# Eleven stages on one core: small weights in one tensor, matrix copies on two engines, deeper buffers in three projections

## The reference

```python
h = tok_mix(x)                 # q,k,v = x@W + b; y = ((d_gamma * (q@k.T)) @ v) @ Wo + bo; prelu. d_gamma 1024x1024
h = concatenate([h, txt], axis=1)
h = h + attention8(ln(h))      # 8 heads of 8, relative bias, softmax, projection with bias
h = h + experts16(ln(h))       # y = z + top 2 of 16 relu experts, layer norm with gamma and beta
h = h + linear_attn(ln(h))     # elu(q)+1, elu(k)+1, projection with bias
u = ln(h)                      # then rms norm, rope, causal attention (4 heads of 16)
u = u + causal(u) @ wo.T
h = h + u + experts8(rms(u))   # top 2 of 8 gated experts
```

## Time and profile before

| | us |
|---|---|
| median of 3 runs | 2847.63 |
| lowest and highest | 2846.12, 2851.1 |
| the profiled execution | 2844.59 |
| its span, first to last instruction | 2842.8 |

### The profile page before, as it was taken

One profiled execution on the slowest core, in us unless ns is written; L12 is line 12 of the kernel. 1 busy time (PEld: TensorE's weight loads), 2 busy tenths in 40 slices (PEclk: granted clock), 3 DMA queues, 4 the chain that ended last, 5 costly groups with the idle time before them and its releaser, 6 DMA issues. The chain is left out here.

```text
span 2842.8 us, 52541 instructions
## 1 busy us (share of the span) xinstructions
PE 2499.5 (88%) x18456; PEld 1092.8 (38%) x18456; DVE 1983.2 (70%) x5070; ACT 1519.3 (53%) x2629; POOL 400.8 (14%) x500
## 2 busy tenths in 40 slices
PE   5988657999999999997499999896679999599999
PEld 3323552333333333333333333564544444423333
DVE  5777667888888888883377776657676765266665
ACT  2331663777777777775144444334656667143443
POOL 1011210000000000002312111222100100411110
PEclk9998666999999999998599999665689999599999
DMA  2101751111111111122500100134441222701100
GB/s 75 23 15 24 239 203 58 48 48 32 48 46 34 48 41 39 48 45 48 111 12 19 25 15 21 48 94 125 154 139 61 81 62 57 155 12 30 30 21 15
DMA packets 272791, 174.02 MB, mean 61 GB/s; under 512 B 225857, under 2 KB 230786, under 8 KB 271282
## 3 DMA queue, kind: packets, MB, share of 16 engines
q1 hardware_dynamic: 262170, 151.59, 19.9%
q0 software_dynamic: 10368, 19.06, 2.2%
HBM read 96.11 MB, written 74.53 MB: 60 GB/s over the span
## 5 line engine op out<-in xcount | busy, mean ns | idle before, releaser
L1674 DVE TENSOR_REDUCE att_mpart<-ps 128x1 f32<-128x512 f32 x1024 | 635.6, 683 | 82.2 <-PE ps L1494 52.0
L1642 ACT ACTIVATE att_p<-ps 128x704 f32<-128x704 f32 x768 | 543.7, 760 | 136.1 <-PE ps L1558 131.8
L1587 PE MATMUL ps<-att_p,att_v 128*9 128x352 f32 x3072 | 300.5, 462 | 0.1
L1494 PE MATMUL ps<-att_kT,att_qT 64*128 64x512 bf16 x1024 | 276.4, 387 | 20.7 <-DMA att_qz<-qt_d 8.3
L1558 PE MATMUL ps<-att_qm,att_kT 64*128 64x352 bf16 x1536 | 251.9, 317 | 10.4 <-ACT att_p L1642 8.0
L1288 DVE TENSOR_REDUCE cau_mpart<-ps 128x1 f32<-128x512 f32 (+5 forms) x384 | 193.4, 552 | 80.3 <-PE ps L1114 60.9
L2419 ACT ACTIVATE mo_act<-ps,mo_b 128x768 f32<-128x768 f32 x176 | 156.3, 901 | 132.4 <-PE ps L2301 126.9
L2572 DVE TENSOR_TENSOR mo_g<-mo_act,ps 128x768 f32<-128x768 f32 x176 | 167.4, 951 | 77.8 <-PE ps L2336 41.2
L1255 ACT ACTIVATE cau_p<-ps 128x704 f32<-128x704 f32 (+6 forms) x272 | 171.5, 660 | 81.7 <-PE ps L1173 49.7
L2971 ACT ACTIVATE mo_act<-ps 128x1024 f32<-128x1024 f32 (+1 forms) x108 | 102.9, 953 | 195.0 <-PE ps L2885 194.8
L1558 PEld LDWEIGHTS ps<-att_qm,att_kT 64*128 64x128 bf16 x1536 | 82.8, 93 | 287.5 <-issue 278.0
(11 more groups left out here) (444 smaller groups left out, 4257.0 us busy)
## 6 DMA issues: line engine op xcount, KB each, us to landing
qs_d<-pre_qs SPq DMA_DIRECT2D x8, 1152.0 KB, 4.4
att_qs<-qs_d SPq DMA_DIRECT2D x32, 288.0 KB, 4.1
qt_d<-pre_qT SPq DMA_DIRECT2D x8, 1056.0 KB, 4.4
kt_d<-pre_kT SPq DMA_DIRECT2D x8, 1056.0 KB, 7.4
att_kT<-kt_d SPq DMA_DIRECT2D x32, 264.0 KB, 2.7
att_qT<-qt_d SPq DMA_DIRECT2D x32, 264.0 KB, 3.1
cqt_d<-cpr_qT SPq DMA_DIRECT2D x8, 1056.0 KB, 4.4
cau_qT<-cqt_d SPq DMA_DIRECT2D x16, 528.0 KB, 4.0
```

Source lines behind the costliest of these rows:

```text
L1494: mm = pe.matmul(ps[:, bank, :], qT[half(s), u, j * P:(j + 1) * P], kT[half(s), u, c * BANK:(c + 1) * BANK], start=True, stop=not near)
L1587: mm = pe.matmul(ps[32 * cg:32 * cg + DV, 7, 0:TH], v[:, u, i, s, :], p[:, r, s, :], start=i < 2, stop=i == FULL - 1)
L1642: e = act.activation(p[:, n % PRING, :, :], ps[:, bank:bank + 2, 0:TH], ACT.Exp)
L1674: red = dve.tensor_reduce(mpart[:, j, s, c:c + 1], ps[:, bank, :], AX.X, ALU.max)
```

## The change

The small weights of the token mix come as one tensor of 128 x 324 and are, like the wide q and k weights, asked for by ACT; SP begins with the rows of image 0 and the matrix. The unit matrices are written in POOL's part of the first stage, and PE waits for them. PE turns four parts of the matrix between the first products, and nine of the sixteen copies are made by ACT. The splitting of x on ACT is cut in two pieces. The copy of txt is issued after the load of image 2.

```diff
+        small = nm.sb("small", [P, W_ALL])
+        wvT, bvb, wo = small[0:C, 0:P], small[0:C, P:2 * P], small[0:C, 2 * P:2 * P + C]
+        bqk, bo, slope = (small[:, 2 * P + C + i:2 * P + C + j] for i, j in ((0, 2), (2, 3), (3, 4)))
...
-        NW = 16 * 12
+        NW = 16 * 2
+
+        ACT_GT = (4, 5, 6, 7, 8, 9, 11, 13, 15)
+
+        def copied(eng, x_):
+
+            if x_ in ACT_GT:
+                eng.wait_ge(S["gt_cp_act"], sum(1 for i in ACT_GT if i <= x_))
+            else:
+                eng.wait_ge(S["gt_cp"], sum(1 for i in range(x_ + 1) if i not in ACT_GT))
...
-            sp.dma_start(wvT[:, :], a["L0_tok_WvT2"]).then_inc(S["w_in"], 16)
-            sp.dma_start(wo[:, :], a["L0_tok_Wo"]).then_inc(S["w_in"], 16)
-            sp.dma_start(bvb[:, :], a["L0_tok_bv_cols"]).then_inc(S["w_in"], 16)
...
-                sp.dma_start(wf[half, 0:V0], a["L0_tok_wqqkk"]).then_inc(S["w_in"], 16)
-                sp.dma_start(bqk[half, 0:1], a["L0_tok_bq"].rearrange("(c o) -> c o", o=1)).then_inc(S["w_in"], 16)
-                sp.dma_start(bqk[half, 1:2], a["L0_tok_bk"].rearrange("(c o) -> c o", o=1)).then_inc(S["w_in"], 16)
-                sp.dma_start(bo[half, :], a["L0_tok_bo"].rearrange("(c o) -> c o", o=1)).then_inc(S["w_in"], 16)
-            sp.dma_start(slope[:, :], a["L0_tok_prelu_a"].broadcast_to([P, 1])).then_inc(S["w_in"], 16)
...
-            sp.dma_start(h_img[:, TX:N, :], a["txt"]).then_inc(S["txt_out"], 16)
...
             load(2, 0)
+            sp.dma_start(h_img[:, TX:N, :], a["txt"]).then_inc(S["txt_out"], 16)
...
+            build_constants(pool, const)
             tidy(pool, const)
             front(0, 0)
...
-            pe.wait_ge(S["w_in"], NW)
-            pe.matmul(ps[:, 4, 0:C], wvT[:, :], wo[:, :], start=True, stop=True)
...
-            for _, part in front_parts:
-                part(0, 0)
-
-            for x_, n in enumerate(GT):
+            def turn_matrix(x_):
...
-                    pe.wait_ge(S["gt_cp"], x_ - 3)
+                    copied(pe, x_ - 4)
...
-            pe.wait_ge(S["gt_cp"], NS)
+
+            pe.wait_ge(const["made"], 2)
+            pe.wait_ge(S["w_in"], NW)
+            pe.matmul(ps[:, 4, 0:C], wvT, wo, start=True, stop=True)
+            pe.matmul(ps[:, 4, C:2 * C], bvb, wo, start=True, stop=True).then_inc(S["wv_mm"], 1)
+            x_turn(0, 0)
+            turn_matrix(0)
+            turn_matrix(1)
+            pe.wait_ge(S["wc_made"], 2)
+            for i in range(4):
+                qk(i)(0, 0)
+                if i < 2:
+                    turn_matrix(2 + i)
+            values(0, 0)
+            for x_ in range(4, NS):
+                turn_matrix(x_)
+            for x_ in range(NS - 4, NS):
+                copied(pe, x_)
             scores(0, 0, 0, False)
...
+            act.dma_start(small[:, :], a["L0_tok_small"]).then_inc(S["w_in"], 16)
+            act.dma_start(wf[:, 0:V0], a["L0_tok_wqqkk"]).then_inc(S["w_in"], 16)
...
+            def copy_matrix(x_):
...
+                act.wait_ge(S["gt_mm"], x_ + 1)
+                act.activation(gamT[:, n // 2, (n % 2) * BANK:(n % 2 + 1) * BANK], ps[:, x_ % 4, :], ACT.Identity)\
+                    .then_inc(S["gt_cp_act"], 1)
...
+
+            split_hi(0, 0)
...
             act.activation(wC[0:C, :], wf[0:C, :], ACT.Identity).then_inc(S["wc_made"], 1)
+            split_mid(0)
             act.wait_ge(S["wr_made"], 1)
...
             front(0, 0)
-            split(1, 1)
+            split_hi(1, 1)
+            for x_ in ACT_GT[:6]:
+                copy_matrix(x_)
+            split_mid(1)
+            for x_ in ACT_GT[6:]:
+                copy_matrix(x_)
...
+            copy_matrix(0)
+            copy_matrix(1)
+            for i in range(4):
+                rest(i)(0, 0)
+                if i < 2:
+                    copy_matrix(2 + i)
+            for i in range(4):
+                stack(i)(0, 0)
+            values(0, 0)
+            for x_ in range(4, NS):
+                if x_ not in ACT_GT:
+                    copy_matrix(x_)
+            copied(dve, NS - 1)
+            copied(dve, NS - 2)
```

```diff
+    OB, RB = 3, 4
...
-            if NO == 2:
-                at_least(sp, S["sum_made"], b - 1)
-            else:
-                at_least(sp, S["ot_mm"], b - 1)
+        def load(eng, b):
+            arrived_heads(eng, b)
+            at_least(eng, S["sum_made" if NO == 2 else "ot_mm"], b - OB + 1)
             for r0, r1 in parts:
-                sp.dma_start(o[r0:r1, par, :, :], o_d[bass.ds(b, 1), :, r0:r1, :].rearrange("b e r n -> r (b e) n"))\
-                    .then_inc(o_in[par], 16)
-
-        def load_rows(sp, b, par):
+                eng.dma_start(o[r0:r1, b % OB, :, :], o_d[bass.ds(b, 1), :, r0:r1, :].rearrange("b e r n -> r (b e) n"))\
+                    .then_inc(o_in[b % OB], 16)
+
+        def sums_in(eng, b):
+            eng.wait_ge(o_in[b % OB], 16 * len(parts) * (b // OB + 1))
+
+        def load_rows(sp, b):
             bi = bass.ds(b, 1)
-            at_least(sp, S["hn_made"], (b - 1) * 2)
-            sp.dma_start(res[:, par, 0:FULL, :], res_b[bi, 0:TX, :].rearrange("b (t p) c -> p (b t) c", p=P)).then_inc(res_in[par], 16)
-            sp.dma_start(res[0:TT, par, FULL, :], res_b[bi, TX:N, :].rearrange("b n c -> (b n) c")).then_inc(res_in[par], 16)
+            x = b % RB
+            at_least(sp, S["hn_made"], (b - RB + 1) * 2)
...
-            for b in range(2, 4):
-                load(sp, b, b % 2)
+            load_rows(sp, 2)
             for b in range(B):
-                if b + 4 < B:
-                    load(sp, b + 4, b % 2)
+                if b + 3 < B:
+                    load_rows(sp, b + 3)
                 if b == B - 3:
                     ahead(sp, const)
                 store(b, b % 2)
-                if b + 2 < B:
-                    load_rows(sp, b + 2, b % 2)
 
...
+            load(act, 2)
             for b in range(B):
                 par = b % 2
+                if b + 3 < B:
+                    load(act, b + 3)
...
-        const["early"][const["building"], "dve"] = {0: zero_tail, 1: lambda dve: measure(dve, 0, 0)}
...
+            act.activation(warm[:, :], const["eye"][:, 0:1], ACT.Sqrt)
             root(0)
```

More of the change, by code:

```diff
@@ L164, in apart, with build_constants @@
     eng.sem_inc(const["passed"], 1)
[L167 to L181, removed]
+def build_constants(pool, const):
+    zeroed, made = const["zeroed"], const["made"]
+    pool.memset(const["eye"][:, :], 0.0).then_inc(zeroed, 1)
+    pool.memset(const["eye16"][:, :], 0.0).then_inc(zeroed, 1)
+    pool.wait_ge(zeroed, 2)
+    for m in (const["eye"], const["eye16"]):
+        pool.affine_select(out=m[:, :], in_=m[:, :], compare_op=ALU.not_equal, fill=1.0, base=0,
+                           pattern=[[-1, P]], channel_multiplier=1).then_inc(made, 1)
 def at_least(eng, sem, value):
@@ L585, in _, with copy_matrix @@
             dve.tensor_tensor(wC[C:P, :], wr[C:P, :], wB[C:P, :], ALU.subtract).then_inc(S["wc_made"], 1)
-            for _, part in front_parts:
-                part(0, 0)
-            for x_, n in enumerate(GT):
+            def copy_matrix(x_):
+                n = GT[x_]
                 dve.wait_ge(S["gt_mm"], x_ + 1)
@@ L3437, in measure, with norm1 @@
                 .then_inc(S["cen_made"], 1)
+        def norm1(dve, b, par):
+            made(dve, b, "root_made")
+            dve.reciprocal(rstd[:, 0, :], sq[:, 0, :]).then_inc(S["rstd_made"], 1)
+            made(dve, b, "rstd_made")
+            if not (isinstance(b, int) and b < 2):
+                dve.wait_ge(u_out[par], (b - par) * 16)
+            made(dve, b, "cen_made")
+            dve.tensor_tensor(u[:, par, :, :], cen[:, :, :], rstd[:, 0, :].unsqueeze(2).broadcast_to([P, NT, C]), ALU.mult)\
+                .then_inc(S["u_made"], 1)
+            dve.tensor_tensor(rsq[:, :], rstd[:, 0, :], rstd[:, 0, :], ALU.mult).then_inc(S["rsq_made"], 1)
+            made(dve, b, "rsq_made")
+            dve.tensor_tensor(msq[:, :], rsq[:, :], stats[:, :, 1], ALU.mult).then_inc(S["msq_made"], 1)
+            made(dve, b, "msq_made")
+            dve.tensor_scalar(var[:, 1, :], msq[:, :], RMS_EPS, None, ALU.add).then_inc(S["var2_made"], 1)
         def zero_tail(dve):
@@ L3449, in fetch @@
             load(sp, 1, 1)
-        const["early"][const["building"], "dve"] = {0: zero_tail, 1: lambda dve: measure(dve, 0, 0)}
+        const["early"][const["building"], "dve"] = {0: zero_tail, 1: lambda dve: measure(dve, 0, 0), 2: lambda dve: norm1(dve, 0, 0)}
         yield fetch
@@ L3660, in _ @@
             not_early(dve, const, "dve")
-            norm1(0, 0)
             norm2(0, 0)
@@ L3702, in step @@
                     measure(dve, b + 2, par)
-                    norm1(b + 2, par)
+                    norm1(dve, b + 2, par)
                 if b >= 2:
@@ L3718, in _ @@
             measure(dve, 1, 1)
-            norm1(1, 1)
+            norm1(dve, 1, 1)
             for b in range(B):
```

104 lines of the change are left out of this document (48 added, 56 removed).

## The result

The changed kernel took **2807.4 us** (median of 4 runs, 2804.8 to 2811.0) against 2849.4 (4 runs, 2846.1 to 2851.7): ratio 0.986, 95% interval 0.9846 to 0.9875, 42.0 us less. The forecast was 53.0 less, 2794.6. The profiled execution has a span of 2805.4 us, 37.4 under the one of before.

What follows compares the result with a forecast made beforehand. It took the start to be bound by DVE's chain behind ten microseconds of asking, and prj and cpj by late residual rows. Savings of 15.4 + 18.6 + 7.2 + 11.8 = 53.0 us from 2847.63 gave 2794.6, range 2783 to 2811.

Steps and rivals of the forecast that it cites:

- A: Whole kernel: the forecast itself, 46 to 60 us off, 2788 to 2802 us; chance 0.60.
- cpj: Third projection: sums start when POOL is free, fronts every 4.5 to 4.7 us; 11.8 us saved, bounds 8 and 15.
- rival B: prj and cpj: transfers bound them, 5.35 us a batch, next stage's loads in the tail; total 42 us, 2806; chance 0.20.
- prj: First projection: earlier sums and rows let PE set the pace, transfers close behind; 18.6 us saved, bounds 13 and 22.
- Start: Kernel's start up to the scores: earlier x and matrix, copies shared with ACT; 15.4 us saved, bounds 11 and 17.
- from there the mix is the same loop: Attention after the scores start: the loop is unchanged, so the 15.4 us saved at the start stay.
- POOL never waits for the rows: prj: with four residual buffers, rows asked three batches ahead, POOL runs at 4.22 us a batch, under PE's 4.56.
- ACT as the asker: Projections: two issues of 0.55 us per batch on ACT stay hidden, costing nothing below about 3 us a pair.
- Rival D: Projections: ACT's issues block its queue, 10.8 us a batch, 37 us a stage, kernel slower at 2907; chance 0.03.
- lpr: Second projection: same PE pace, but POOL's fills finish earlier and the next stage starts sooner; 7.2 us saved, bounds 4 and 9.5.
- the last hn ends 12.3 us later, and 0.9 us for the next stage's loads: cpj's tail: from front(7) at 2452 to the last hn at 2464.3, then 0.9 us, ending at 2465.2.

Runs made afterwards that it cites:

- experiment 4: Changed kernel with sums asked for by SP instead of ACT: ahead of each step's rows, 2830.84 us (0.9937); in the old kernel's place, 2813.88 us (0.9871).

## Why the prediction was right, and by how much each step was off

The verdict (faster, within 2783 to 2811) held in each session, and in its steps A, the forecast, is what the profiles show, but for the tail of cpj. The number is another matter. A's own band was 46 to 60 us off. The 42.0 measured are below it, and to the microsecond those of rival B (42 us, 2806). That is chance: B takes its 11 us from prj and cpj, and there the profile is 4.5 us short of the forecast; most of the rest is lin, which no step had. With fewer of lin's slow images, as in the second profile, the span is 51.1 us shorter, within A. By its own steps:

**Start, 15.4 forecast; 18.1 to 18.9 measured at the first g in the three profiles of the change, 16.3 to 19.2 in all eleven with this start.** X's turn, forecast 9.6, came at 9.63. From x's turn to DVE's last front part I carried 17.2 + 0.7 us; it took 15.7 (9.63 to 25.36). The last turns and copies then took 3.1 us to the scores (25.36 to 28.45), against 3.9 with the low clock's 0.8. At the start of prj 13.7 to 14.9 us were left (11.8 to 17.3 in the eleven). The step "from there the mix is the same loop" stands within that spread, which the forecast did not have.

**prj, 18.6 forecast (13 to 22), 18.3 to 19.0 measured** to the last hn. Front(7) came 35.1, 33.7 and 34.1 us after the first sum in the three profiles, against 34.0 forecast and 36.4 by rival B. The total is thus A's, and the way there is partly B's: PE held its 4.56 us only up to front(5), and the last two steps (5.44 and 6.42 us, 5.06 and 5.39, 5.63 and 5.27) waited for residual rows, which in the first profile took 7.1 to 9.2 us to land, at a DMA share of 1.03. "POOL never waits for the rows" was wrong; the forecast had 1.6 us of slack over PE's pace, which about covered it. In cpj, where POOL adds no bias, the fronts came every 4.50 us at the same share, and B's pace falls there.

**ACT as the asker, nothing forecast, nothing lost.** Its issues took 0.45 to 0.78 us each between copies that stayed at 0.60. Rival D is refuted. What the step missed is that SP as asker would have cost 6 us (experiment 4): I priced who asks as a cost only, not as part of prj's and cpj's gain.

**lpr, 7.2 forecast (4 to 9.5), 7.5 to 8.2 measured.** By the rule on DVE and POOL (the Trainium skill, SBUF — State Buffer, "Who interferes with whom") DVE would wait out the fill and the gain be 4 us. The small operation beside the fill did take 0.80 us instead of 0.17 and ended 0.03 us after the fill, so the trace agrees; the price was 0.6 us and not 3, since the fill had only 0.8 us to go.

**cpj, 11.8 forecast (8 to 15), 7.4 to 7.8 measured: the term that was mis-sized, and just outside its bounds.** Up to front(7) the step is right (31.2 us after the first sum forecast, 30.5 measured). It failed in "the last hn ends 12.3 us later, and 0.9 us for the next stage's loads". From front(7) to the last hn it took 17.9 us. I had freed the tail of its residual rows and had not asked what is late next: the store of hn(5), asked for behind the experts' 1.5 MB of w1 and w3, which frees the buffer of hn(7). The trace of before had it already: there the last residual rows landed at 2476.28 and this store at 2475.62, 0.66 us ahead, so with earlier rows alone this last wait could end only 0.66 us sooner. SP stood 5.51 us in the issue of these rows:

```profile
2466.90 0.76 SPq L1786 DMA_DIRECT2D hidden<-cpj_hn  x1
...
2468.60 5.51 SPq L1757 DMA_DIRECT2D cpj_res<-u_d  x1
```

In the changed kernel the store was asked for at 2429.99 and landed 9.2 us later. Rival B had a part of this right: that the next stage's first weights land in the tail. It gave them 3 us in prj and in cpj; in cpj they cost 5.6, by way of this store. Prj has the wait too (2.1 to 2.8 us), but with the third buffer it gained only 0.8. The third buffer brought cpj to 43.4 us, where the forecast had 43.5 to the last hn, and the stage behind it then waited for SP's queue, so cpj's missing 4 us came back only when the small transfers were moved as well.

**What no step had: lin.** The sum counted every untouched stage as fixed. Lin gave +9.9, +2.7 and +10.2 us in three profiles of the same code. With the second of these the span is 51.1 us shorter, against 53.0 forecast; with the others 36.3 and 37.4. In the first profile, from 53.0 to 37.4 us, lin takes 9.9, cpj 4.1, the start 1.7, and the other stages and lpr nothing to speak of. So what the median gained less than forecast is for the most part lin's slow images, and then cpj's tail. That a change of the start and of projections sets lin back by way of PE's clock is not shown: the code alone does not fix it, and why the changed kernel's medians lie at 2793 and 2807 while those of the kernel before agree within 2.8 us stays open. Of the kernel before there is one profile, so its own spread (2841.7 to 2857.4 in 35 executions) is not traced to a stage.

## What to carry to other kernels

When a wait goes, follow the buffer that the waiting instruction writes as well as those that it reads: what is late next is often the store that frees it, and behind that the queue of the engine that asks. The trace of before tells when each of them landed: here the second-latest was 0.66 us ahead of the latest. Ask for the few small transfers that a stage's first instruction needs before its large weights. And before a difference of 10 us in 2800 is put down to an edit, take a second profile of the same code and compare stage by stage: a stage that was not touched can hold it all.

## What the runs showed of the hardware that I had not expected

- PE's granted clock changed between 2.4 and 1.2 GHz image by image within one stage, in six patterns over fourteen profiles, and differently in executions of one program. With four fast images of eight lin took 112.8 to 113.3 us, with two 122.7 to 123.1.
- One issue of a transfer on SP took 4.9 to 5.7 us when 1.5 MB of weights had been asked for just ahead on that queue, against a median of 0.51 us over all of SP's issues; it held all that SP had to ask for after it. It is not only these weights: each profile has six to eleven issues of over 3 us on SP, as behind the 4 MB matrix at the start (4.9 us) and at residual rows of prj (4.08 us). None of the 36 issues of sums on ACT took over 0.78 us.
- With 16 engines at a share of 1.03 and 221 GB/s for 10 us PE still had its sums in time in cpj: a full share alone did not make the transfers the bound. What came late at such a share were prj's residual rows, 7.1 to 9.2 us after the ask and not 2.6 to 3.9.
